# Node-matrix powers as fp32r products of halves, feature-matrix powers between the transposes, and small loads on ScalarE's queue: a change to the setup of a two-layer graph kernel

## The reference, cut to what matters

```python
    def _L0_gnn_ref(x, adj_mx, alpha_train, w, d, fc_in_w, fc_in_b, vt):
        N_STEPS = 8
        x0 = jax.lax.stop_gradient(x)
        h = jnp.einsum('bnd,ed->bne', x, fc_in_w) + fc_in_b
        alph = jax.nn.sigmoid(alpha_train)[:, None]
        d_clamped = jnp.clip(d, 0.0, 1.0)
        w_eff = w * d_clamped @ w.T
        dt = jnp.float32(SPATIAL_SCALE / N_STEPS)
        def euler_step(h, _):
            ax = jnp.einsum('nm,bmd->bnd', adj_mx, h)
            f = alph * 0.5 * (ax - h) + h @ w_eff - h + x0
            return (h + dt * f, None)
        h, _ = jax.lax.scan(euler_step, h, None, length=N_STEPS)
        return h
...
    h = jnp.maximum(_layernorm(x, axis=-1), 0.0)
    x = x + _L0_gnn_ref(h, adj, L0_gnn_alpha_train, L0_gnn_w, L0_gnn_d, L0_gnn_fc_in_w, L0_gnn_fc_in_b, 0)
    h = jnp.maximum(_layernorm(x, axis=-1), 0.0)
    x = x + _L1_gnn_ref(h, adj, adj, ...)
    return x
```

## Time and profile before

| what | value |
|---|---|
| median of 3 runs | 996.07 us (994.97, 996.07, 1000.45) |
| profiled execution, its own time | 1006.55 us |
| span of its instructions | 1004.8 us |
| mean granted TensorE clock | 0.963 |
| busy share of the span: TensorE | 92% |
| DVE, ACT, POOL | 61%, 53%, 31% |
| first row of the rounds' preparation (L721) starts | 62.66 us |

### The profile page before, as it was taken

The page is one execution under the profiler, slowest core; times in us unless marked ns, Lnnn a source line. Parts: engine busy times, 40 slices in busy tenths (PEclk is TensorE's granted clock), DMA queues, the critical chain, the costliest instruction groups (busy, mean ns, idle before and its releaser), DMA issues.

```text
span 1004.8 us, 20057 instructions
## 1 busy us (share of the span) xinstructions
PE 928.6 (92%) x7078; PEld 750.6 (75%) x7078; DVE 615.0 (61%) x2003; ACT 534.7 (53%) x1176; POOL 314.9 (31%) x421
## 2 busy tenths in 40 slices
PE   5998999999999999989599999999999999888993
PEld 4555889999999999978477777777777777666773
DVE  3753323333333333434478888888888888876786
ACT  2232232222222222221388888888888888885575
POOL 0001101111111111213134455444454454323786
PEclk8887999999999999999799999999999999998998
DMA  3000000000000000001354445555545444410122
GB/s 92 1 1 10 11 1 11 10 18 13 10 10 10 10 10 10 12 1 60 67 133 121 128 127 127 127 127 127 127 127 127 126 114 118 112 39 2 43 63 64
DMA packets 47218, 61.54 MB, mean 61 GB/s; under 512 B 4377, under 2 KB 22050, under 8 KB 47138
## 3 DMA queue, kind: packets, MB, share of 16 engines
q1 hardware_dynamic: 47138, 60.51, 23.4%
HBM read 39.53 MB, written 20.97 MB: 60 GB/s over the span
## 4 chain that ended last, share of the span: by engine, by line
PE 16%; DVE 10%; POOL 9%; issue 9%; ACT 6%; DVEq 0%; POOLq 0%; ACTq 0%
PE bank L1568 4%; DVE prob L1738 3%; PE bank L1588 3%; PE bank L1632 2%; ACT prob L1679 2%; POOL z_gain L301 2%; POOL z_norm L305 2%; POOL x_bo L1512 2%; PE bank L1555 2%; POOL rstd_b L186 1%; DVE z_std L282 1%; PE bank L333 1%; PE bank L337 1%; POOL rstd L186 1%; ACT probT L1668 1%
## 5 line engine op out<-in xcount | busy, mean ns | idle before, releaser
L1679 ACT ACTIVATE prob<-prob,low 128x512 f32<-128x512 f32 x256 | 184.0, 719 | 53.2 <-DVE low L1738 51.3
L1738 DVE CUSTOM_DVE_ANT_0 prob<-bank,mask 128x512 f32<-128x512 f32 x256 | 171.2, 683 | 26.8 <-PE bank L1555 25.3
L1568 PE MATMUL bank<-ident,prob 128*128 128x128 f32 x1024 | 163.2, 282 | 12.5 <-ACT probT L1668 12.5
L1568 PEld LDWEIGHTS bank<-ident,prob 128*128 128x128 f32 x1024 | 114.9, 142 | 58.8 <-issue 31.5
L1555 PE MATMUL bank<-k_stack,q_stack 128*128 128x512 f32 x256 | 123.8, 485 | 9.9 <-DVE low L1738 5.0
L1668 ACT ACTIVATE probT<-bank 128x512 f32<-128x512 f32 x176 | 102.4, 582 | 3.1 <-PE bank L1568 1.6
L1065 DVE TENSOR_TENSOR T_lo<-bank,T_hi 128x512 fp32r<-128x512 f32 x48 | 33.0, 688 | 111.9 <-ACT T_hi L903 111.9
L903 ACT ACTIVATE T_hi<-bank 128x512 fp32r<-128x512 f32 x48 | 28.4, 591 | 134.5 <-PE bank L813 91.4
L601 POOL TENSOR_SCALAR var_eps<-mv 128x4 f32<-128x4 f32 x16 | 3.6, 226 | 298.1 <-DVE mv L1018 298.1
L909 ACT ACTIVATE Sq<-bank,trace_inv 128x512 fp32r<-128x512 f32 x64 | 43.9, 686 | 92.5 <-PE bank L736 92.5
L1588 PE MATMUL bank<-probT,v 128*32 128x128 f32 x2048 | 82.7, 280 | 4.4 <-DVE probT L1725 1.7
(11 more groups left out here) (241 smaller groups left out, 1930.8 us busy)
## 6 DMA issues: line engine op xcount, KB each, us to landing
k_stack<-bounce_q SPq DMA_DIRECT2D x64, 256.0 KB, 4.9
q_stack<-bounce_k SPq DMA_DIRECT2D x64, 256.0 KB, 7.5
bounce_q<-k_parts SPq DMA_DIRECT2D x16, 512.0 KB, 2.8
bounce_k<-q_parts SPq DMA_DIRECT2D x16, 512.0 KB, 3.2
x_in<-in_x_dram SPq DMA_DIRECT2D x16, 256.0 KB, 2.8
out_dram<-probT SPq DMA_DIRECT2D x16, 256.0 KB, 2.3
A<-in_adj_dram SPq DMA_DIRECT2D x4, 256.0 KB, 3.4
W1s<-in_L_gnn_W_dram SPq DMA_DIRECT2D x1, 128.0 KB, 2.3
```

The lines of the kernel that those rows point to most:

```text
L1568: last = pe.transpose(psum[2 + u % 2][:, mt * P:(mt + 1) * P], prob[u % RING][:, mt * P:(mt + 1) * P], ident[:, :])
L1679: act.activation(prob[u % RING][:, :], prob[u % RING][:, :], ACT.Exp, bias=low[:, u % TURNED:u % TURNED + 1], scale=-1.0, accum_out=row_su ...
L1738: dve.tensor_tensor_reduce(prob[u % RING][:, :], psum[u % 2][:, :], mask[:, u // HEADS, :], 1.0, 3e38, ALU.add, ALU.min, low[:, u % TURNED ...
```

## The change

1. Small loads: the five small transfers leave SP's queue and are issued by ACT, ahead of its table load, in the order w, d, alpha, fc_b, fc_w. There is a semaphore of its own for w and for fc_w, and DVE and ACT wait for the other three only.
2. TensorE transposes w and forms W before it waits for A. The powers 1 to 4 stand behind the four tiles of A's transposes, 5 to 8 behind those of Pn's, one each. The fc products follow at once, ahead of P2T.
3. P2T and P3T are formed by `node_power`: three fp32r products for each float32 product, 48 for each power. For that Pn is split too: the high half by ACT, the low half by POOL, into the memory of the `T` tiles, which are not yet in use.
4. PT and P2T are split tile by tile straight from PSUM (ACT the high half, DVE the low half), and are not stored whole. Where the vector product for U needs PT, POOL adds the halves again (`PT_sum_ready`).
5. DVE's order changes: S*0.5, the cast to Sq and the mask lie between the low halves of P2T, and the 36 steps of B come after the start of the squaring. A, Pn and PT lie in y's memory, which is written from round 1 on.

```diff
-                sp.dma_start(alpha_in[:, :], alpha.rearrange("(t p) -> p t", p=P),
-                             allow_slow_non_contiguous=True).then_inc(small_loaded, 16)
-                sp.dma_start(w_in[:, :], w).then_inc(small_loaded, 16)
...
+                for mt in range(NT):
+                    pool.wait_ge(Pn_hi_ready, mt + 1)
+                    pool.tensor_tensor(out=Pn_parts[1][:, mt, :], in0=Pn[:, mt, :],
+                                       in1=Pn_parts[0][:, mt, :].bitcast(F32), op=ALU.subtract
+                                       ).then_inc(Pn_lo_ready, 1)
+                pool.wait_ge(PT_lo_ready, NT)
+                pool.tensor_tensor(out=PT[:, :, :], in0=PT_parts[0][:, :, :].bitcast(F32),
+                                   in1=PT_parts[1][:, :, :].bitcast(F32), op=ALU.add).then_inc(PT_sum_ready, 1)
                 scales(0, 0)
...
+                def node_power(mt, parts, psum_sem):
+                    for k in range(NT):
+                        for n, (left, right) in enumerate(products(Pn_parts, parts)):
+                            last = pe.matmul(psum[mt][:, :], left[:, k, mt * P:(mt + 1) * P], right[:, k, :],
+                                             start=k == 0 and n == 0, stop=k == NT - 1 and n == 2)
+                    last.then_inc(psum_sem, 1)
...
+                pe.wait_ge(loaded, 16 * NT)
                 for mt in range(NT):
...
+                    adj_turned(mt)
+                    power(mt + 1)
+                for mt in range(NT):
+                    node_turned(mt)
+                    power(NT + mt + 1)
+
+                pe.wait_ge(fc_loaded, 16)
                 pe.wait_ge(power_ready, STEPS + 1)
...
+                pe.wait_ge(Pn_lo_ready, NT)
+                pe.wait_ge(PT_lo_ready, NT)
+                for mt in range(NT):
+                    node_power(mt, PT_parts, P2_psum)
...
+                pe.wait_ge(PT_lo_ready, 2 * NT)
                 for mt in range(NT):
...
+                    node_power(mt, P2T_parts, P3_psum)
...
             @block.scalar
             def _(act):
-                act.wait_ge(small_loaded, 16 * 5)
+                act.dma_start(w_in[:, :], w).then_inc(w_loaded, 16)
+                act.dma_start(d_in[:, :], d.rearrange("(p o) -> p o", o=1)).then_inc(small_loaded, 16)
...
+                for mt in range(NT):
+                    if mt == NT - 1:
+                        enter(0, 0)
+                    act.wait_ge(P2_psum, mt + 1)
+                    act.activation(P2T_parts[0][:, mt, :], psum[mt][:, :], ACT.Copy).then_inc(PT_hi_ready, 1)
...
+                def turned_lo(mt, parts, count):
+                    dve.wait_ge(PT_hi_ready, count)
+                    dve.tensor_tensor(out=parts[1][:, mt, :], in0=psum[mt][:, :],
+                                      in1=parts[0][:, mt, :].bitcast(F32), op=ALU.subtract).then_inc(PT_lo_ready, 1)
```

More of the change, by code:

```diff
@@ L453, in layer0 @@
         x0_parts = [[sb(f"x0_{part}{i}", [P, NT, D], F32R) for part in ("hi", "lo")] for i in range(2)]
-        T_parts = [[[sb(f"T{m}_{part}{i}", [P, N], F32R) for part in ("hi", "lo")] for m in range(GROUP)]
+        T_all = sb("T_all", [P, 2 * GROUP * 2, N], F32R)
+        T_parts = [[[T_all[:, (i * GROUP + m) * 2 + part, :] for part in range(2)] for m in range(GROUP)]
                    for i in range(2)]
+        Pn_parts = (T_all[:, 0:NT, :], T_all[:, NT:2 * NT, :])
         C2 = sb("C2", [P, NT, D])
         Y1 = sb("Y1", [P, NT, D])
-        with ExitStack() as early:
-            A, Pn, PT, P2T = (tensor(early, n, [P, NT, N]) for n in ("A", "Pn", "PT", "P2T"))
+        A, Pn, PT = (y[:, i * NT * N:(i + 1) * NT * N].rearrange("p (t n) -> p t n", n=N) for i in range(3))
         PT_hi, P2T_hi, PT_lo, P2T_lo = (sb(n, [P, NT, N], F32R) for n in ("PT_hi", "P2T_hi", "PT_lo", "P2T_lo"))
@@ L637, in _, with adj_turned @@
             def _(pe):
-                pe.wait_ge(ident_ready, 1)
-                pe.wait_ge(loaded, 16 * NT)
-                for mt in range(NT):
+                def adj_turned(mt):
                     for nt in range(NT):
@@ L645, in _, with node_turned @@
                     last.then_inc(adjT_psum, 1)
-                pe.wait_ge(small_loaded, 16 * 5)
-                pe.transpose(psum[4][:, 0:D], w_in[:, :], ident[:, :]).then_inc(wT_psum, 1)
-                pe.wait_ge(wT_ready, 2)
-                pe.matmul(psum[5][:, 0:D], wT[:, :], dwT[:, :], start=True, stop=True).then_inc(weff_psum, 1)
-                pe.wait_ge(P_ready, 2 * NT)
-                for mt in range(NT):
+                def node_turned(mt):
+                    if mt == 0:
+                        pe.wait_ge(P_ready, 2 * NT)
                     pe.wait_ge(adjT_ready, mt + 1)
@@ L658, in _, with power @@
                     last.then_inc(PT_psum, 1)
-                for k in range(1, STEPS + 1):
+                def power(k):
                     pe.wait_ge(power_ready, k)
@@ L678, in _ @@
                                      powers[:, k, 0:D], start=True, stop=True)
-                last.then_inc(FW_psum, 1)
-                pe.wait_ge(P2_ready, NT)
+                last.then_inc(setup_psum, 1)
+                pe.wait_ge(Pn_lo_ready, NT)
+                pe.wait_ge(PT_lo_ready, NT)
+                for mt in range(NT):
+                    node_power(mt, PT_parts, P2_psum)
+                pe.wait_ge(S_ready, 2)
+                pe.wait_ge(B_step, 1)
+                pe.matmul(SQ_BANK[:, 0:1], ones[:, :], row_sum[:, :], start=True, stop=True).then_inc(setup_psum, 1)
+                pe.wait_ge(PT_sum_ready, 1)
                 pe.wait_ge(U_ready, 2)
@@ L687, in _ @@
                                          start=k == 0, stop=k == NT - 1)
-                last.then_inc(U_psum, 1)
+                last.then_inc(setup_psum, 1)
+                pe.wait_ge(PT_lo_ready, 2 * NT)
                 for mt in range(NT):
-                    for k in range(NT):
-                        last = pe.matmul(psum[mt][:, :], Pn[:, k, mt * P:(mt + 1) * P], P2T[:, k, :],
-                                         start=k == 0, stop=k == NT - 1)
-                    last.then_inc(P3_psum, 1)
+                    node_power(mt, P2T_parts, P3_psum)
                 pe.wait_ge(P3_ready, NT)
@@ L872, in _ @@
                 for mt in range(NT):
+                    act.wait_ge(P_ready, NT + mt + 1)
+                    act.activation(Pn_parts[0][:, mt, :], Pn[:, mt, :], ACT.Copy).then_inc(Pn_hi_ready, 1)
+                for mt in range(NT):
                     act.wait_ge(PT_psum, mt + 1)
-                    act.activation(PT[:, mt, :], psum[mt][:, :], ACT.Copy).then_inc(PT_ready, 1)
-                for mt in range(NT):
-                    act.wait_ge(P2_psum, mt + 1)
-                    act.activation(P2T[:, mt, :], psum[mt][:, :], ACT.Copy).then_inc(P2_ready, 1)
+                    act.activation(PT_parts[0][:, mt, :], psum[mt][:, :], ACT.Copy).then_inc(PT_hi_ready, 1)
                 def enter(b, s):
@@ L897, in _ @@
                     act.activation(P3T[:, mt, :], psum[mt][:, :], ACT.Copy).then_inc(P3_ready, 1)
-                act.wait_ge(P2_ready, NT)
-                act.activation(P2T_parts[0][:, :, :], P2T[:, :, :], ACT.Copy).then_inc(PT_hi_ready, 1)
                 def T_hi(m, b, s):
@@ L972, in _ @@
                                       ALU.mult).then_inc(P_ready, 1)
+                power_out(1)
                 for t in range(NT):
```

156 lines of the change are left out of this document (79 added, 77 removed).

## The result

The changed kernel takes 986.78 us (median of four runs, 985.23 to 988.23) against 998.21 us for the kernel before, run beside it on the same chip (four runs, 994.97 to 1000.45). The ratio is 0.9877, with an interval of 0.9844 to 0.9911. Two later measurements of the same pair, on two chips, gave 0.9862 [0.9827, 0.9896] and 0.9852 [0.9825, 0.9880]. The forecast was 988.0, with a chance of 0.84 that the kernel gets faster by over 0.5%.

What follows compares the result with a forecast made beforehand. Only the setup up to L721 counts: latencies bind TensorE until 23.80, then its own work and clock. Front 1.9, P2T 3.5 and P3T 2.8 save 8.2 us, taking the median from 996.07 to 988; range 984 to 992.5.

Steps and rivals of the forecast that it cites:

- The products: P2T and P3T: 48 fp32r products take 10.9 us against 13.7 for 32 float32 instructions, saving 2.8 each at full clock.
- The rival by which these products are no quicker: P2T and P3T: fp32r products no quicker than 0.29 us, leaving only 1.9 and 0.7 saved; 993.5 us, chance 0.04.
- The clock in P2T, U and P3T: Low clock costs P2T 0.7 us instead of 1.4 and P3T 2.45 as before; U unchanged.
- Rival (a): Setup: full clock from the transposes on, no fall in U; L721 at 49, saved 13.6, 982.5 us; chance 0.10.
- The front: Setup up to P2T: P2T starts at 24.0, 0.2 later, but with the 2.1 us fc products done; saved 1.9.
- their upper bound of 7.8: Start of setup: small loads taken in at 6.0, with bounds 4.5 and the 7.8 of the kernel before.
- the walk: Front: queues followed with measured durations; eight groups of transposes and power at 1.3 us, 10.4 in all, last power copied by 20.2.
- powers and transposes with waits between them are what the clock fell in before: Front: the reason for taking the fc products at 3.8 us, near their low-clock 4.2 rather than 2.1.
- The rule on queues: Small loads beside A: a second issuer saves only issue time, so they gain less; A pushed back to 7.3, hidden.
- What was hidden: Splits, sum of halves and B steps finish under TensorE's work before P2T and P3T, with margins of 1.4 to 3 us.
- the forecast's slow bound: Pn's low halves on POOL before P2T: at 1.64 us each, ready at 20.9 instead of 19.5, still hidden.
- The first round: After the broadcast: P2T's low halves and B's copy no longer lie there; counted as no gain.

Runs made afterwards that it cites:

- the last version: Changed kernel with x's loads held back, one tile of A's transposes before W's product, S's addition and other DVE and ACT work moved later; 984.27 us, ratio 0.9843.
- front and U: Changed kernel with U's products behind P3T, x's loads held back, one tile of A's transposes before W's product, S's addition later; 991.27 us, ratio 0.9893.
- before again: The kernel before the change, unedited, timed and traced a second time; 1000.55 us, ratio 0.9983 to its neighbour.
- x held back: Changed kernel with SP issuing the two x loads only once d, alpha and the bias have landed; 988.06 us, ratio 0.9860 to the kernel before.
- loads on SP: Changed kernel with the five small loads back on SP's queue behind A; 992.04 us, ratio 0.9889 to the kernel before.
- chain: Changed kernel with the eight powers of W in one chain behind the transposes of Pn; 994.43 us, ratio 0.9919 to the kernel before.

## Why the prediction was right

**The products.** Right in size. fp32r products of this operand stand 0.23 us apart at full clock, P2T's 48 take 10.97 (forecast 10.9 without low clock), and the experiment with one float32 product each gives back 2.8 and 2.9. The rival by which these products are no quicker is out.

**The clock in P2T, U and P3T.** Mis-sized by 2 us in all. The forecast gave P2T 0.7 of low clock; it had none, because the clock had been full since 14. It took U as unchanged at 4.41; the fall came 0.3 and 0.9 behind U's end in two traces and 0.5 ahead of it in the third, and not in its middle, so that U took 3.57, 3.57 and 3.81. It gave P3T 2.45; it had half of 3.4, so 1.7. The place of the fall was right to a microsecond or two. Its cause is only half shown: it went with U when U was moved behind P3T, but with a front 3 us shorter it stayed away though U stood where it had. Rival (a) put the full clock through U and P3T as well; it held through U only, and in two of the three traces.

**The front.** The forecast of 24.0 for P2T stands against 22.45, from errors of both signs. A's transposes start at 9.62 and not at 7.4, 2.2 late, because the small loads were taken in at 6.0 and came at 8.05. That is beyond their upper bound of 7.8, which took "no earlier than now" for the worst. Against that, the walk priced each group and power at 1.3, as at the low clock; from 13.7 on they took 0.88, so that the way from the first transpose to the fc products was 10.8 instead of 12.8. The two waits of the walk, 0.7 for the scalings and 1.1 for S, came as 0.3 and 1.6. And the fc products took 2.0, not 3.8. The step that failed in reasoning is "powers and transposes with waits between them are what the clock fell in before". Before, it fell in a chain of powers alone (at 19.7, with the chain running from 16.4); it falls again where the chain is put back (at 19.0, within the wait for S), and with powers and transposes interleaved it does not in any trace, though TensorE waits there too (1.5 to 1.6 for S).

**The rule on queues.** The Trainium skill, DMA: Bandwidth & Descriptors, section "Issuing engines are not separate DMA queues", says that transfers of different issuers interleave on the same engines. The traces agree (A 4.6 us instead of 3.2, b 5.9 instead of 2.6; about 0.9 of b's is x's loads behind A), and it should have had more weight: the forecast took the second queue as a gain of 1.8 for the small loads, and it is a loss of 0.9.

**What was hidden.** Right, with less margin than said. POOL's low halves began at 15.75, 1.5 later than walked, and took 6.54. That sum is the forecast's slow bound (four of 1.64), but not its mechanism: three took 1.27 and one, beside S's addition, 2.85. They were ready at 22.29, 0.16 before P2T instead of three; PT's low halves at 21.49 (21.6 forecast), the sum of the halves at 26.9 (26.8 to 28.2), P2T's last low half at 35.42, 1.7 before P3T, the B steps from 37.3 to 44.7. With POOL's start where it was, powers or fc products quicker by more than 0.2 would have waited for POOL; the last version, with the shorter front, has S's addition moved away from these subtractions.

**The first round.** Forecast at nothing, it gave 2.3 on average. After the change P2T's low halves and B's copy no longer lie there, and there is less low clock. Which of the two it is, the traces tell without a further run, for the low clock of a trace differs from one execution to the next. For the changed kernel from the broadcast to the first C, in its first and its third trace (as above; the clock is the third number from the end):
```profile
50.61:88.00 37.39, 30.99 (x128) 23.43 (x129) 12.28 (x36) 9.35 (x16) 3.35 (x5) 0.86 0.03 8
...
50.21:89.50 39.29, 33.54 (x128) 25.08 (x129) 12.26 (x35) 9.35 (x16) 3.35 (x5) 0.78 0.02 7
```
A clock of 0.86 over 37.4 us is 10 us at 0.50, and 0.78 over 39.3 is 17. The same reading of all twelve traces:

| clock, broadcast to first C | traces | us |
|---|---|---|
| 0.75 | before; float32 products; front and U | 40.8; 41.0; 41.0 |
| 0.78 | before again; U behind P3T; the third of the changed kernel; the last version | 39.6; 39.4; 39.3; 39.3 |
| 0.82 | x held back | 37.8 |
| 0.86 | the first two of the changed kernel; loads on SP; chain | 37.4, 37.1; 37.4; 37.6 |

At equal clock the stretch is as long in the kernel before as in the versions of the changed one, within 0.3 us. So the work that left the first round is worth nothing there, as forecast, and the 2.3 is low clock, which these two and three traces happened to have more or less of. Whether the change lowers it on average they are too few to say.

So 8.2 was forecast from the setup, and 11.3 measured. The change itself was forecast too small, by 3.1 us in the setup, and by 3 to 8 in the three differences of medians. The forecast median of 988.0 still lies close, and that is in part luck: it starts from 996.07, the lowest of the medians from 996 to 1004 that the kernel before has here.

## What to carry to other kernels

A chain of small dependent products costs twice, its own waits and the clock behind them; put independent work, here transposes, between its links. A second DMA queue brought only its first load in sooner while large ones were under way, and those behind it later; holding back the later large loads helped. To issue the small loads ahead of the large ones on one queue was not tried. When a setup is shortened, follow the gain to the first output of the main loop: here a further 4.1 to 4.6 us won before the broadcast left 2.3 to 4.1 behind it, and the difference is low clock. The three traces of the changed kernel differ by 1.8 there in the same way, so compare stretches at equal granted clock.

## What the runs showed of the hardware

With U's 32 products of one column ahead of P3T, which keep TensorE busy without a gap, the clock fell within about a microsecond of their end in six traces (38.0, 37.5 and 36.5 in those of the changed kernel). With them behind P3T it fell 1.5 to 1.8 behind their end, in the first round (51). In one version, where they end at 34.2, it did not fall until 50, and in another it fell behind a wait of 2.94 with no U ahead. What else it takes is open. It also rose while TensorE did nothing but float32 transposes and small products, at 12.6 to 14.1 us in the three traces of the changed kernel.

POOL and DVE held each other up. POOL's subtraction of 128x512 takes 1.27 us by itself and took 2.85 to 2.87, in all seven traces with that order, when DVE's addition of two inputs from SBUF (2.28 by itself) was already under way, ending 1.13 after it. POOL's sum over 128x2048 takes 4.6 and took 6.61 in the same place, ending 4.5 after the addition. Where POOL's subtraction had started first, DVE's addition took 3.28. So in these traces the one that started later got next to nothing done until the other had ended. The GPSIMD Engine Reference of the Trainium skill, section "Key points", names this contention; the runs give it that size.

In the rounds, which none of these edits touch, most stretches of low clock begin in about the same places, but their number and length vary. The changed kernel has the one from 68 on with 10.2, 10.2 and 13.7 us, the one near 107 with 6.8, none and 3.4, and an extra one at 53.6 in its third trace alone. The span of the unchanged kernel moved by 9.5 us with them (0.963 and 0.970 mean clock). What sets their length stays open, and with it why part of the last version's gain is lost there.
